# Sixteen-head attention of an eight-stage kernel: six split products a head in half of the array's rows, columns and rows of different heads issued in turn

## The reference, cut to what matters

```python
x = x + _L0_xattn_ref(...)     # att0, 8 heads
x = x + _L0_ffn_ref(...)       # ffn0
x = x + _L1_xattn_ref(_layernorm(x, axis=-1), ctx_768, ...)   # att1
x = x + _L1_ffn_ref(...)       # moe1
...
def _L1_xattn_ref(x, y, Wq, bq, Wk, bk, Wv, bv, W1, b1, W2, b2):
    q = (x @ Wq + bq).reshape(B, N, NUM_HEADS, HEAD_DIM)      # 16 heads of 8
    k = (y @ Wk + bk).reshape(B, M, NUM_HEADS, HEAD_DIM)
    v = (y @ Wv + bv).reshape(B, M, NUM_HEADS, HEAD_DIM)
    scores = jnp.einsum('bnhd,bmhd->bhnm', q, k) * scale
    attn = jax.nn.softmax(scores, axis=-1)
    out = jnp.einsum('bhnm,bmhd->bnhd', attn, v).reshape(B, N, IMAGE_DIM)
    h = jax.nn.relu(out @ W1 + b1)
    return h @ W2 + b2
```

## Time and profile before

| | us |
|---|---|
| median of 3 runs | 785.33 |
| lowest and highest | 781.67 and 785.69 |
| span of the profiled execution | 779.4 |
| TensorE matmuls busy (ends modelled) | 638.1 |
| VectorE busy | 490.8 |
| ScalarE busy | 386.3 |
| GpSimd busy | 302.9 |
| VectorE's maxima, L975, 256 times | 169.7 |
| ScalarE's exponentials, L1743, 256 times | 148.6 |
| TensorE's rows, L2083, 512 matmuls | 102.8 |
| TensorE's columns, L2095, 512 matmuls | 100.8 |
| TensorE's averages, L2111, 1024 records | 71.9 |

### The profile page before, as it was taken

How to read it: one execution, slowest core, us unless ns; L and a number is a source line. 1 busy time by engine, 2 the same in 40 slices (tenths; PEclk the granted TensorE clock), 3 DMA queues, 4 the chain that set the end, 5 groups by cost and what they waited for, 6 DMA issues and landing times.

```text
span 779.4 us, 15312 instructions
## 1 busy us (share of the span) xinstructions
PE 638.1 (82%) x4712; PEld 467.2 (60%) x4712; DVE 490.8 (63%) x1428; ACT 386.3 (50%) x860; POOL 302.9 (39%) x456
## 2 busy tenths in 40 slices
PE   2688788889999887899977777748898777699997
PEld 1355666556665544899944555437796566456665
DVE  4678666877778753556867785636657665455443
ACT  5356465466666565466624655335776444232221
POOL 4435355443333036162747644372545730000000
PEclk9999999999999999699976998777999999699999
DMA  6263423333333200144354441012455100223331
GB/s 185 60 158 97 112 73 90 90 94 88 90 95 89 78 19 38 53 130 119 103 138 114 120 128 42 16 41 83 126 143 157 51 11 1 70 69 105 98 95 56
DMA packets 93575, 68.71 MB, mean 88 GB/s; under 512 B 9800, under 2 KB 84424, under 8 KB 93272
## 3 DMA queue, kind: packets, MB, share of 16 engines
q1 hardware_dynamic: 89400, 59.34, 27.4%
q0 software_dynamic: 4096, 8.40, 3.5%
HBM read 30.94 MB, written 14.35 MB: 58 GB/s over the span
## 4 chain that ended last, share of the span: by engine, by line
PE 36%; DVE 8%; issue 6%; DMA 4%; POOL 3%; ACT 3%; SPq 1%; ACTq 0%; DVEq 0%; POOLq 0%
PE ps L2396 7%; PE ps L2406 4%; PE ps L2434 4%; PE ps L2436 4%; PE ps L2447 4%; DVE negmax L975 2%; DMA late<-outputs_moe,placed 2%; PE ps L2111 1%; PE ps L2095 1%; PE ps L2035 1%; PE ps L2390 1%; PE ps L2083 1%; PE ps L2289 1%; POOL gathered L1600 1%; DVE x_sb L1295 1%
## 5 line engine op out<-in xcount | busy, mean ns | idle before, releaser
L975 DVE TENSOR_REDUCE negmax<-ps 128x2 f32<-128x512 f32 x256 | 169.7, 686 | 87.5 <-PE ps L2083 86.8
L1743 ACT ACTIVATE exps<-ps 128x512 f32<-128x512 f32 x256 | 148.6, 598 | 100.7 <-PE ps L2095 99.9
L2083 PE MATMUL ps<-stack 96*128 96x256 bf16 x512 | 102.8, 295 | 26.7 <-DVE negmax L975 23.4
L2095 PE MATMUL ps<-stack 99*128 99x256 bf16 x512 | 100.8, 287 | 19.2 <-DMA stack<-maxt 17.7
L1600 POOL DMA_INDIRECT gathered<-z,placed x64 | 62.4, 975 | 63.3 <-PE ps L2390 28.6
L1618 POOL DMA_INDIRECT late<-outputs_moe,placed x64 | 62.1, 971 | 50.8 <-issue 15.8
L2095 PEld LDWEIGHTS ps<-stack 99*128 99x128 bf16 x512 | 44.2, 102 | 60.2 <-DMA stack<-maxt 24.4
L2083 PEld LDWEIGHTS ps<-stack 96*128 96x128 bf16 x512 | 47.9, 103 | 51.5 <-DVE negmax L975 39.4
L2111 PE MATMUL ps<-exps,values 128*32 128x256 f32 x1024 | 71.9, 398 | 1.3 <-ACT exps L1743 1.0
L1984 ACT ACTIVATE gated<-ps 128x512 f32<-128x512 f32 x36 | 21.5, 597 | 83.1 <-PE ps L2436 83.1
L2406 PE MATMUL ps<-pack_moe,ht 128*128 x368 | 60.1, 288 | 1.3 <-ACT ht L1970 0.8
(11 more groups left out here) (225 smaller groups left out, 1257.4 us busy)
## 6 DMA issues: line engine op xcount, KB each, us to landing
stack<-qk_parts SPq DMA_DIRECT2D x168, 128.0 KB
stack<-weights_t SPq DMA_DIRECT2D x32, 256.0 KB, 3.3
outputs_moe<-y_kept SPq DMA_DIRECT2D x92, 64.0 KB
ht<-gathered SPq DMA_DIRECT2D x44, 128.0 KB, 2.2
pack_moe<-in_moe SPq DMA_DIRECT2D x11, 256.5 KB, 3.9
pack_moe<-in_moe SPq DMA_DIRECT2D x6, 429.5 KB, 4.1
gathered<-y_kept SPq DMA_DIRECT2D x10, 256.0 KB, 3.6
pack_moe<-in_moe SPq DMA_DIRECT2D x1, 1732.0 KB, 7.4
```

What stands on the lines that cost most here:

```text
L975: dve.tensor_reduce(negmax_of[b % 2][:, :, h:h + 1].rearrange("p t h -> p (t h)"), ps[:, h % 2, :].rearrange("p (t k) -> p t k", t=2), AX, ...
L1743: nc.scalar.activation(exps[:, i, :], ps[:, 2 + h % 2, :], ACT.Exp, scale=scale)\
L2083: last = pe.matmul(ps[:, h % 2, t * T:(t + 1) * T], st[0:MAXROW, h, 0, t * P:(t + 1) * P], st[0:MAXROW, h, 1, :], start=True, stop=True)
L2095: last = pe.matmul(ps[:, 2 + h % 2, t * T:(t + 1) * T], st[0:MAXROW + 3, h, 1, t * P:(t + 1) * P], st[0:MAXROW + 3, h, 0, :], start=True, ...
```

## The change

`att1` uses the six slots of the other stages, so a head needs 6 x 8 = 48 partitions and its maxima three more. Two heads now stand above each other in `stack`: even heads at partitions 0 to 50, odd ones at 64 to 114, in places 8 to 15 of the tile. The matmuls contract over 48 and 51 partitions instead of 96 and 99. In a beat that has a column and a row of `att1`, `rows_beside_columns` waits for both and then issues first half of the column, first half of the row, second half of the column, second half of the row. A spread becomes 12 DMAs of 64 KB instead of 9 of 128 KB, and the maxima go in two DMAs instead of one. The memset on GpSimd and its semaphore are gone; ScalarE writes ones once into partitions 32 to 63 and 96 to 127 of the new places.

```diff
-    "att1": [(0, 0), (0, 1), (1, 0), (1, 1), (0, 2), (2, 0), (1, 2), (2, 1), (2, 2)],
+    "att1": [(0, 0), (0, 1), (1, 0), (1, 1), (0, 2), (2, 0)],
...
-MAXROW = 96
+MAXROW = {"att0": 96, "att1": 48, "att2": 96}
+HALF = P // 2
+HALVES = {"att0": 1, "att1": 2, "att2": 1}
+FIRST_PLACE = {"att0": 0, "att1": 8, "att2": 0}
...
                 if s == "att1" and p < 3:
-                    sp.wait_ge(rows_padded, p + 1)
                     sp.wait_ge(rows_filled, 3)
...
-                    sp.dma_start(stack[i][j:j + n * (dh - 1) + 1:n, 0:nh, :, :],
-                                 qk_parts[:, qa:3 + kc + 1:3 + kc - qa, :]).then_inc(stack_in[i], 16)
+                    for half in range(HALVES[s]):
+                        at = half * HALF + j
+                        sp.dma_start(stack[i][at:at + n * (dh - 1) + 1:n, to, :, :],
+                                     qk_parts[half::HALVES[s], qa:3 + kc + 1:3 + kc - qa, :]).then_inc(stack_in[i], 16)
...
-                        sp.dma_start(stack[i][MAXROW:MAXROW + 3, 0:H[sm], 0, :], maxt[0:3 * H[sm], :])\
-                            .then_inc(maxrow_in[i], 16)
+                        for half in range(HALVES[sm]):
+                            at = half * HALF + MAXROW[sm]
+                            sp.dma_start(stack[i][at:at + 3, to, 0, :], maxt[half:3 * H[sm]:HALVES[sm], :])\
+                                .then_inc(maxrow_in[i], 16)
...
-                        if u == 5 and valid(p) and s == "att1" and p < 3:
-                            wait(pool, "cols_psum", s, p - 3)
-                            pool.memset(stack[buf(s, p)][0:MAXROW, 0:8, 1, :].bitcast(F32), 0.0).then_inc(rows_padded, 1)
...
             def fill_rows(i):
-                rows = stack[i][64:MAXROW, 8:16, :, :].rearrange("p h a t -> p (h a t)").bitcast(F32)
-                nc.scalar.activation(rows, zt[64:MAXROW, 0, 0:1].to_broadcast([MAXROW - 64, 8 * T]), ACT.Copy)\
-                    .then_inc(rows_filled, 1)
+                write_ones(slice(32, HALF), i, slice(8, 16))
+                write_ones(slice(32 + HALF, P), i, slice(8, 16)).then_inc(rows_filled, 1)
...
+            def row_half(s, m, h, t):
+                at, k = half_place(s, h)
+                st = stack[buf(s, m)][at:at + MAXROW[s], k, :, :]
+                return pe.matmul(ps[:, h % 2, t * T:(t + 1) * T], st[:, 0, t * P:(t + 1) * P], st[:, 1, :], start=True, stop=True)
...
+            def column_half(s, a, h, t):
+                at, k = half_place(s, h)
+                st = stack[buf(s, a)][at:at + MAXROW[s] + 3, k, :, :]
+                return pe.matmul(ps[:, 2 + h % 2, t * T:(t + 1) * T], st[:, 1, t * P:(t + 1) * P], st[:, 0, :], start=True, stop=True)
...
+            def rows_beside_columns(s, a, h, m, g):
+                wait_columns(s, a, h)
+                wait_rows(s, m, g)
+                for t in range(2):
+                    column = column_half(s, a, h, t)
+                    row = row_half(s, m, g, t)
+                column.then_inc(sem["cols_psum"], 1)
+                row.then_inc(sem["rows_psum"], 1)
...
+                if [st for st, _, _ in col + row] == ["att1", "att1"] and (col[0][2] + row[0][2]) % 2:
+                    rows_beside_columns(*col[0], *row[0][1:])
+                else:
+                    for st, b, h in col:
+                        columns(st, b, h)
+                    for st, b, h in row:
+                        rows(st, b, h)
```

More of the change, by code:

```diff
@@ L299, in build @@
         maxrow_ones = ctx.enter_context(nc.semaphore("maxrow_ones"))
-        rows_padded = ctx.enter_context(nc.semaphore("rows_padded"))
         rows_filled = ctx.enter_context(nc.semaphore("rows_filled"))
@@ L602, in stack_total @@
         def stack_total(s, b):
-            return sum(16 * len(SLOTS[st]) for st in uses(s, b))
+            return sum(16 * len(SLOTS[st]) * HALVES[st] for st in uses(s, b))
         def ranks_at(s, g):
@@ L671, in maxrow_total, with half_place @@
         def maxrow_total(s, b):
-            return 16 * len(uses(s, b))
+            return sum(16 * HALVES[st] for st in uses(s, b))
+        def half_place(s, h):
+            return h % HALVES[s] * HALF, FIRST_PLACE[s] + h // HALVES[s]
         block = ctx.enter_context(nc.Block())
@@ L2074, in project_o, with wait_rows @@
                 last.then_inc(sem["proj_psum"], 1)
-            def rows(s, m, h):
-                st = stack[buf(s, m)]
+            def wait_rows(s, m, h):
                 if h == 0:
@@ L2081, in rows, with wait_columns @@
                 wait(pe, "max_done", s, m, h - 2)
-                for t in range(2):
-                    last = pe.matmul(ps[:, h % 2, t * T:(t + 1) * T], st[0:MAXROW, h, 0, t * P:(t + 1) * P],
-                                     st[0:MAXROW, h, 1, :], start=True, stop=True)
-                last.then_inc(sem["rows_psum"], 1)
-            def columns(s, a, h):
-                st = stack[buf(s, a)]
+            def row_half(s, m, h, t):
+                at, k = half_place(s, h)
+                st = stack[buf(s, m)][at:at + MAXROW[s], k, :, :]
+                return pe.matmul(ps[:, h % 2, t * T:(t + 1) * T], st[:, 0, t * P:(t + 1) * P], st[:, 1, :], start=True, stop=True)
+            def wait_columns(s, a, h):
                 if h == 0:
@@ L2143, in beat @@
                 kv = ct[:, 0, :] if s == "att0" else ctxt_sb[:, p % B * T:(p % B + 1) * T]
-                for st, b, h in due(flow, step, u, "a", column_beats):
-                    columns(st, b, h)
-                for st, b, h in due(flow, step, u, "m", row_beats):
-                    rows(st, b, h)
+                col = list(due(flow, step, u, "a", column_beats))
+                row = list(due(flow, step, u, "m", row_beats))
+                if [st for st, _, _ in col + row] == ["att1", "att1"] and (col[0][2] + row[0][2]) % 2:
[5 more added lines that the diff above has]
+                        rows(st, b, h)
                 if u == 0 and valid(p):
```

22 lines of the change are left out of this document (16 added, 6 removed).

## The result

On one chip, in alternation, the changed kernel took **794.42 us** (median of 6 runs, 789.02 to 800.88), the kernel before 785.38 us (6 runs): ratio **1.0102, interval 1.0068 to 1.0136**. Slower by 1.0%; the forecast of 780.8 and its range up to 790.0 both missed it. The ratio leaves out the run of 800.88, which lies 1.5% above the kernel's fastest. A later comparison gave 1.0166 (1.0099 to 1.0234).

A forecast was written before the change was run, and what follows sets the result against it. The prediction took TensorE to set the pace, with a fixed transfer chain once a batch. Pairs -4.55, maxima +2.0 and handover -2.0 summed to -4.55 us: 780.8 us, 8-in-10 range 774.5 to 790.

The forecast's parts named there:

- The sum: Whole kernel: pairs -4.55, maxima transfers +2.0, handover -2.0, together -4.55 us.
- 0.75 us a stretch for the pairs: 16-head attention, from `ot`'s projection to the next turn of the maxima: gain in five of seven stretches, 0.4 in two.
- 0.25 for the second DMA: Maxima transfer: sent in two DMAs, the first column comes 0.25 us later a batch, 2.0 us over eight batches.
- The sign that the prediction named for being wrong: Prediction wrong if waits for VectorE's maxima stay small, a period falling by 2 us, or the granted clock drops within the stage.
- That the halves run at once: Paired beats on TensorE: a beat's four matmuls take 0.22 instead of 0.44 us; bounds 0.22 and 0.44.
- The changes of tiling: TensorE, ends of paired runs: 10 a period at 0.09 us, 0.9 us a period; bounds 0 and 2.0.
- First column to the projection of `ot`: This part of a period gains nothing, VectorE and ScalarE pacing it: projection at 8.07 us after, 8.13 before.
- The chain of the maxima: Turn of the maxima to first column: copy as long as before, second transfer 0.25 us later, 3.86 instead of 3.61 us.
- The handover: From 8 to 16 heads: earlier, smaller spread less alternating tilings, 2.0 us gained, bounds 0 and 3.9.
- the forecast's early part: First batch's spread at the handover: 1.6 to 2.24 us of the wait go, perhaps up to 1.7 us of slow clock.
- the alternation of tilings: After the handover: whole-array 8-head columns alternate with half-array 16-head rows, some 20 changes at 0.09, 1.8 us lost.
- my third rival: The clock falls in the idle ahead of each first column: 1.15 us a fall, slower at 789 us, chance 0.13.

The follow-up runs named there:

- e4: Changed kernel with up to three float32 whole-array matmuls, results overwritten, ahead of each batch's first columns; 0.9957 of the kernel before.
- e2: Kernel before with six slots in 48 and 51 partitions, all in the lower half, never paired, one maxima DMA; 1.0603 of the kernel before.
- e9: Changed kernel with the maxima's turn ahead of its beat's columns and rows and the copy ahead of the exponentials, 16-head stage only; 1.0016 of the kernel before.
- e10: Kernel before with the maxima's turn ahead of its beat's columns and rows and the copy ahead of the exponentials, 16-head stage only; 0.9993.
- e1: Kernel before with the six-slot product list alone, still whole array (96 and 99 partitions), one maxima DMA; 0.9985 of the kernel before.
- e7: Kernel before with the extra matmuls of e4 ahead of each batch's first columns; 0.9948 of the kernel before.
- e6: Changed kernel run again, unaltered, on one chip with later variants; 1.0166 of the kernel before.
- e8: Changed kernel with the extra matmuls of e4, over 48 partitions in place of 128; 1.0018 of the kernel before.
- e15: Changed kernel with the extra matmuls of e4 and the 16-head row maxima taken over half the keys; 0.9911 of the kernel before.
- e3: Changed kernel with each beat's two columns issued first, then its two rows, instead of by turns; 1.0114 of the kernel before.
- e5: Kernel before with the row maxima sent in two DMAs and nothing else; 1.0047 of the kernel before.

## Why the prediction failed

Two steps of the prediction failed. The sum put the clock at nothing, and falls cost 7.6 us in three steps; with most of them gone in e4 the ratio is 0.9957, with the second step's left in. And it counted 0.75 us a stretch for the pairs less 0.25 for the second DMA, 1.5 us for the three steps that kept the full clock, of which nothing came. The sign that the prediction named for being wrong, a clock that drops within the stage, is the one that was seen.

- **That the halves run at once** was right: pairs start 0.12 us apart, a beat's four matmuls take 0.23 us (predicted 0.22). The mechanism held; what it was to bring did not.
- **The changes of tiling were priced too low.** The prediction took 0.09 us an end, 10 a period, 0.9 us. After has 0.09 at the averages too, but where float32 matmuls over the whole array stand between pairs, the first of them is alone with its weight load as well (L2251's first load starts with it at 227.69, where L2209's had started 0.11 us ahead of it, and the eight last 1.16 us instead of 1.05). With L2251 between, the pairs stand 1.41 us apart (227.37 to 228.78), 0.22 of it for the pair itself; before it was 1.33 (225.74 to 227.07) with 0.44 for columns and rows. So there and back costs 1.19 - 0.89 = 0.30 us, and 0.29 in e2, against 0.22 that the pairs of a beat save. The Trainium skill ("TensorEngine Tiling (Array Packing)", Key Properties) says that a change of mode drains the engine. The trace agrees, with 0.09 us at each change, and adds the exposed load. With these, and a new wait of 0.18 us for `hid`, the stretch from the projection of `ot` to the turn of the maxima takes 5.92 us (223.40 to 229.32): 0.18 less than before, where 0.75 was forecast. This is the term of the sum that was furthest off at the full clock.
- **First column to the projection of `ot`**: forecast to stay (8.07), measured 7.80, a gain of 0.3 us that I had not given it.
- **The chain of the maxima** was forecast at 3.86 us and is 4.38. The transfer has the predicted size: 3.13 us from issue to column (212.47 to 215.60) against 3.06. The copy has not. It "is as long as before", I wrote, and so is its length; but its start is bound by the two exponentials ahead of it on ScalarE, not by the turn. In the earlier trace rows it starts 0.41 us after the turn, now 0.85. The columns of that beat start, the exponentials follow, then the copy: 1.4 us from the beat's first column in both kernels (227.07 to 228.46 before, 228.78 to 230.18 after). So what the beat saves ahead of the turn turns into waiting behind it. With copy and turn ahead of the beat 0.6 us of the fifth step come back in e9; but 0.5 come back in the kernel before too (e10), where the copy was bound in the same way.
- **At the full clock** the sum of the three is +0.26 us a period instead of -0.5; counted by engine, TensorE is busy 1.45 us less and idle 1.71 us more. The idle time stands ahead of the first column (1.15, before 0.44), ahead of `nd` and `ot` (0.27 and 0.44), and four times for a maximum or for `hid` (0.18 to 0.29 each, 0.9 in all).
- **The handover** gained 2.4 us up to the first rows (129.10 instead of 131.48), no wait and no slow clock there: a bit over the forecast's early part. But the first step is 1.2 us longer although its clock is 1.00 where it was 0.91, so the alternation of tilings (forecast 1.8) cost 1.2 us and whatever the slow clock had cost there before; no run separates the two. What was not forecast is the second step, 2.6 us for the clock at 0.69. Part of this is the execution that was profiled: the kernel before has 1.00 there in its one, but e1, e7 and e10, all whole-array, have 0.91, 0.92 and 0.91 and steps of 19.98, 20.08 and 19.82 us instead of 19.61.
- **The clock** was my third rival, at 789 us and a chance of 0.13, and it is what happened. Two terms of it were too small. The idle time ahead of the first columns grows from batch to batch, 0.57 us to 2.07, and is 1.69 and more in the last four, where 1.56 by starts was forecast for all; the late copy is part of it. And I priced a fall at 1.15 us, from the short stretch at the handover; in after a step with a fall is 2.4 to 2.6 us longer, since TensorE comes back to 2.4 GHz only after 7 to 14 us. The forecast argued from the earlier trace rows, where 1.67 us of idle time brought no fall. That was one execution and no rule: e1, the same kernel with six slots, falls behind 1.69 us at the same place. The Trainium skill ("TensorE: Matmul & The Clock Gate", Part 1) has the clock go by how busy TensorE has been. The falls behind the waits agree with that; e2 does not by its records, busy 28.28 us of 28.67 at a clock of 0.65.

What stays open: where in the stage the falls lie that the kernel before has in most of its runs and e7 has not; whether the filling, the changes of tiling or the waits alone make the changed kernel fall more often; what starts the fall at 149 us, which comes in every kernel with half-filled rows (e4, e6, e8, e9 too, for about 14 us) in a stretch where rows stand without columns, and in e1, e7 and e10 for about 4; and how much of e15's remaining difference is the second DMA.

## What to carry to other kernels

Packing two products into the halves of the array is worth its matmul time only in runs: here each visit of a float32 whole-array matmul between pairs costs 0.3 us, more than the 0.22 that the pairs of a beat save. Before making the busiest engine's work shorter, follow the once-a-batch chain from it and ask which engine's queue its next link really stands behind: if that is not the shortened engine, the gain becomes idle time, here ahead of a DMA, and idle time on TensorE can cost its clock. And look at the granted clock of each stretch first when a change takes work away and the time rises; a few matmuls that do nothing, put into the wait, tell in one run whether it is the clock, if the unchanged kernel is run with them too: here they gave it half a per cent.

## What the runs showed of the hardware

- Two halves of the array run at once even when their matmuls are issued one half after the other: in e3, column, column, row, row started at 197.39, 197.51, 197.40 and 197.51.
- A change between whole array and halves with float32 matmuls between costs 0.29 us (e2: 0.96 against 0.67) to 0.30 (after: 1.19 against 0.89) there and back, 0.09 of it each way as at the column strips, the rest at the first whole-array matmul, whose weight load nothing covers.
- With products over 48 and 51 partitions, one at a time (e2), TensorE stayed at a mean granted clock of 0.53 to 0.65 for three steps of 29 us in which it was busy 96 to 99% of the time, then at 1.00 for three more; with 96 and 99 partitions and the same order (e1) it was at 0.90 to 1.00.
- The length of one wait does not settle whether the clock falls behind it: in whole-array kernels it fell behind 1.68 us (e5) and 1.69 (e1), not behind 1.67 (the kernel before) and 1.88 (e5). The runs of the kernel before differ in their mean clock, 0.914 to 0.937 in 27 runs; with one to three float32 matmuls in the wait ahead of a batch's first columns eleven runs have 0.929 to 0.941 (e7). In the changed kernel these left one fall of 4 us between 163 and 310 us where four had been (e4), over 48 partitions as over 128 (e8).
- Two DMAs of 12 KB issued 0.80 us apart (after: 212.47 and 213.27) let the first column start 3.13 us after the first issue (215.60), one of 24 KB 2.81 us after it: the second costs 0.3 us, not 0.8.
